# Two-layer kernel: four query and key products moved to the first layer's end, a store handed to the attention, the rotation's second half in fp32r

## The chip, the cores and the metric

The kernel runs on one core of one Trainium2 chip. The metric is the device time in microseconds (us) of one execution; the kernel before takes 1761.54 us, the median of three runs (1761.18 to 1764.38).

## The reference

The input x has 2 sequences of 1024 tokens with 512 features, and all arithmetic is float32. Two layers follow each other:

```
xn = layernorm(x)
x  = x + L0_attn(xn) + L0_ffn(xn)   # L0_attn: rank-8 scan and rank-8 feed-forward
                                    # L0_ffn : fwht(silu(xn@W1.T) * (xn@W3.T)) @ W2.T, hidden size 2048
xn = layernorm(x)
x  = x + L1_attn(xn) + L1_ffn(xn)   # L1_attn: causal attention, 16 heads of 32
                                    # L1_ffn : gated, two of each four hidden values kept
```

`fwht` is a Walsh-Hadamard transform over the 2048 hidden features. As it is linear, the kernel applies it once to W2 instead of to the hidden values: it rotates W2.

## The kernel before

The program is four phases, each ended by a barrier of all engines: `layer_zero` (the whole first layer), `project_qkv` (queries, keys and values of the second), `attention`, and `layer_end`. TensorE has no full-precision product at full rate. So nearly every product is made of three in the format fp32r: an operand a is split into a rounded part (hi) and the rest (lo), and the product is hi·hi + hi·lo + lo·hi. Weights are split on POOL: one instruction rounds, the next subtracts. Activations are rounded on ACT and subtracted on DVE. Everything is written by hand, in order, one program for each engine, with semaphores between them; all DMAs are issued by SP, in order. There is no planner.

**layer_zero.** 2048 tokens are four quarters of 512. A unit u = 4g + t is hidden group g (512 of the 2048 hidden features, in four pieces c) for quarter t. A unit has `hidden` (per c 12 products for the gate and 12 for the other factor), and one unit later `output` (4 tiles of 12 products). At `before_half` TensorE does side work, among it the rotation of W2. Its first half, `rotate`, stores its result to memory (`w_half_turned`); its second half is `turn_down(g, c)` (L369 to L380): 16 products of the 128x128 matrix `turn_w[:, 1]` with a 128x512 block `raw`, in plain fp32, in units 4g+1 before pieces c = 1 and 3. The blocks come through a ring of 3 slots `raw`, which the gate and up weights use too; a slot is refilled when the rotation of it is done. ACT and DVE turn the result into `d_hi` and `d_lo`.

At the end of the layer the normalised rows of quarters 2 and 3 are transposed by `turn_last` (L573), each followed by ACT (x_hi) and DVE (x_lo). Between the two quarters `keep_going(24)` (L558) issues 24 small fp32 products whose result nobody reads.

**project_qkv.** For each of 4 groups of heads ("quads") there are 8 jobs of 12 products: two blocks of 128 rows of the query and key weights (index i) times four quarters of x. ACT evicts a job (`val`, L1247), DVE splits it into `qk` (L1277, L1279), and SP stores `qk` to memory for each two jobs (L1150). The first quad is written out, the other three are a loop; between them stand 16 jobs for the values (L1231), with weights `raw_v` split by POOL (L1201, L1203). At its start this phase loads `raw_w`, `bias`, `scale` and `raw_v`, and POOL splits `raw_w` (L1190, L1193) before the first job. At its end SP waits for both chains of stores of `qk` before it comes to the barrier (L1181).

**attention** loads `stack` from the stored q and k pairs and starts with scores (L1429).

Of the kernel before, what the change touches and what calls it, by code (L numbers as in the profile page):

```python
# [6 lines left out]

# [16 lines left out]
NC = 4  # L24
# [42 lines left out]
def layer_zero(nc, t, ident, x_hi, x_lo, spare, half_turned, parked):  # L67
# [14 lines left out]
    with ExitStack() as ctx:  # L82
# [8 lines left out]
        raw = sb("raw", [P, RING, FLAT])  # L91
# [23 lines left out]
        turn_w = sb("turn_w", [P, 2, P])  # L115
        stats = sb("stats", [P, NT, 6])
# [27 lines left out]
        p_out = ps("p_out", [P, 2, W])  # L144
        p_side = ps("p_side", [P, 2, W])
# [11 lines left out]
        rot_done, rot_copied, tok_normed = sem("rot_done"), sem("rot_copied"), sem("tok_normed")  # L157
        d_turned, d_round, d_split = sem("d_turned"), sem("d_round"), sem("d_split")
# [35 lines left out]
        def _(sp):  # L194
# [92 lines left out]
            for k in range(39, 48):  # L287
                load_raw(k)
            for q in range(QUARTERS):
                store_res(q)  # L290
# [4 lines left out]
        def _(pool):  # L295
            step = Tally(pool_step)

            def split(k, hi, lo):
                landed(pool, k)
                pool.tensor_scalar(hi, raw[:, k % RING], 1.0, 0.0, ALU.mult, ALU.add).then_inc(step.up(), 1)  # L300
                pool.wait_ge(step.sem, step.n)
                pool.tensor_tensor(lo, raw[:, k % RING], hi.bitcast(F32), ALU.subtract).then_inc(raw_split, 1)

# [38 lines left out]
            pool.memset(q_w[:].bitcast(F32), 0.0).then_inc(rows_done, 1)  # L342
            for g in range(1, NG):
                split_gu(g)

        @block.tensor
        def _(pe):
# [227 lines left out]

            tail = (p_gate[:, 0], p_gate[:, 1], p_up[:, 0], p_up[:, 1])
# [515 lines left out]
def project_qkv(nc, wqk, wv, qk_bias, qk_scale, masks, x_hi, x_lo, qk_dram, v_dram, stack, v_first, mask):  # L1092
# [10 lines left out]
    with ExitStack() as ctx:  # L1103
        sb, ps, sem = alloc(nc, ctx)
        raw_w = sb("raw_w", [P, 2, KD, P])
        w_hi = sb("w_hi", [P, 2, KD, P], F32R)
        w_lo = sb("w_lo", [P, 2, KD, P], F32R)
# [8 lines left out]
        qk = sb("qk", [P, 2, 2, S], F32R)  # L1116
        v = sb("v_out", [P, BANKS, QUADS, 4, 2, E], F32R)
        p_job = ps("p_job", [P, BANKS, W])
# [3 lines left out]
        w_loaded = [sem(f"w_loaded{i}") for i in range(2)]  # L1122
        w_rounded = [sem(f"w_rounded{i}") for i in range(2)]
        w_split = [sem(f"w_split{i}") for i in range(2)]
        w_biased = [sem(f"w_biased{i}") for i in range(2)]
        job_done, job_used = sem("job_done"), sem("job_used")
        qk_rounded, qk_split, v_rounded, v_split = sem("qk_rounded"), sem("qk_split"), sem("v_rounded"), sem("v_split")
        qk_stored = [sem(f"qk_stored{i}") for i in range(2)]
# [7 lines left out]
        def _(sp):  # L1136
# [5 lines left out]
            def body(it, last):  # L1142
                if not last:
                    for i in range(2):
                        load_w(it + 1, i)
                for n in range(4):

                    pair = 2 * (n % 2) + n // 2
                    sp.wait_ge(qk_split, QK * it + 2 * n + 2)
                    sp.dma_start(qk_dram[4 * it + pair].rearrange("h p n -> p h n"), qk[:, n % 2].bitcast(F32))\  # L1150
# [28 lines left out]
            for i in range(2):  # L1179
                sp.wait_ge(qk_stored[i], 16 * 2 * QUADS)  # L1180
# [3 lines left out]
        def _(pool):  # L1184
            def split_w(quad, i, first=False):
                pool.wait_ge(w_loaded[i], 16 * (quad + 1))
                if not first:

                    pool.wait_ge(job_done, QK * (quad - 1) + 4 * i + 4)
                pool.tensor_tensor(w_hi[:, i].rearrange("p k m -> p (k m)"), raw_w[:, i].rearrange("p k m -> p (k m)"),  # L1190
                                   one[:, :].to_broadcast([P, D]), ALU.mult).then_inc(w_rounded[i], 1)
                pool.wait_ge(w_rounded[i], quad + 1)
                pool.tensor_tensor(w_lo[:, i], raw_w[:, i], w_hi[:, i].bitcast(F32), ALU.subtract).then_inc(w_split[i], 1)  # L1193
# [3 lines left out]
            for i in range(2):  # L1197
                split_w(0, i, True)
# [10 lines left out]
        def _(pe):  # L1209
            def body(it, first):  # L1210
                for m in range(QK):
                    i = m // 4
                    if m % 4 == 0:
                        pe.wait_ge(w_split[i], it + 1)
                    if not (first and m < BANKS):
                        pe.wait_ge(job_used, QK * it + m + 1 - BANKS)
                    t = m % 4
# [20 lines left out]
        def _(act):  # L1238
            def body(it, first):
                for m in range(QK):  # L1240
                    i = m // 4
                    act.wait_ge(job_done, QK * it + m + 1)
                    if m % 4 == 0:
# [18 lines left out]
        def _(dve):  # L1262
            def body(it, first):
                for m in range(QK):
                    if m in (0, 4):
                        i = m // 4
                        if not first:

                            dve.wait_ge(job_used, QK * (it - 1) + m + 4)
# [6 lines left out]
                    hi, lo = (qk[:, m // 2 % 2, half, part * W:(part + 1) * W] for half in range(2))  # L1276
# [18 lines left out]
def attention(nc, mask, stack, v, ident, qk_dram, v_dram, o_dram, total, o_both, o_stored, load_next):  # L1295
# [40 lines left out]
    with ExitStack() as ctx:  # L1336
        sb, ps, sem = alloc(nc, ctx)
        prob = [sb("prob0", [P, 2, QB, W]), sb("prob1", [P, 2, QB, S])]
# [18 lines left out]
        def width_of(r):  # L1357
            return (r + 1) * P

# [24 lines left out]
        def _(sp):  # L1384
# [26 lines left out]

            for it in range(QUADS - 1):
# [5 lines left out]
        def _(pe):  # L1418
# [15 lines left out]
            def turn(it, h, j):  # L1434
# [6 lines left out]
                for i in range(c0 // P, QB):  # L1441
                    mm = pe.transpose(p_turn[:, (BL * h + j) % TB, i * P:(i + 1) * P],  # L1442
                                      prob[g][:, h % 2, i, kb * P:(kb + 1) * P], ident[:, :])
# [20 lines left out]
        def _(act):  # L1464
            def exp(it, h, r):
# [5 lines left out]
                act.activation(prob[r // QB][:, h % 2, r % QB, 0:width_of(r)], p_score[:, r % 2, 0:width_of(r)], ACT.Exp,  # L1471
# [434 lines left out]
def two_layers(nc, t, out):  # L1906
# [7 lines left out]
    with ExitStack() as ctx:  # L1914
# [6 lines left out]
        phase(nc, layer_zero, t, ident, x_hi, x_lo, spare, half_turned, parked)  # L1921
        total = sb("total", [P, HEADS * NT])
        raw = sb("raw1", [P, RING, KD * P])
        handed = alloc(nc, ctx)[2]
        raw_in = [handed(f"raw1_in{i}") for i in range(RING)]
        o_stored = [handed(f"o_stored{i}") for i in range(4)]

# [4 lines left out]
        with ExitStack() as middle:  # L1932
            sb1 = alloc(nc, middle)[0]
            o_both = sb1("o_both", [2 * E, len(o_stored), W])
            stack = sb1("stack", [P, 2, 2, 2, S], F32R)
            v = sb1("v", [P, B, S // P, 4, 2, E], F32R)
            mask = sb1("mask", [P, 2, P], BF16)
            phase(nc, project_qkv, t["wqk"], t["wv"], t["qk_bias"], t["qk_scale"], t["masks"], x_hi, x_lo, qk_dram,
                  v_dram, stack, v, mask)
            phase(nc, attention, mask, stack, v, ident, qk_dram, v_dram, o_dram, total, o_both, o_stored, load_first_blocks)  # L1940
# [74 lines left out]
```

## Time and profile before

| | |
|---|---|
| median of three runs | 1761.54 us |
| the profiled execution, its own time | 1764.71 us |
| its span, first to last instruction | 1762.5 us |
| TensorE products busy | 1701.5 us, 97% |
| DVE, ACT, POOL busy | 59%, 42%, 14% |
| layer_zero | up to about 642 us |
| project_qkv | about 642 to 788 us |
| attention | about 788 to 1186 us |
| layer_end | about 1186 us to the end |

All times in the document's rows are microseconds from the start of the span. A busy share near 100% says only that products follow each other with little idle time; what is to be gained is in the idle times left, in work on TensorE that is dearer than it has to be, and in work that nobody reads.

### The profile page before, as it was taken

To read this page: it belongs to the slowest core of one execution; us is meant where nothing else is said; L and a number is where in the kernel's file an instruction comes from. 1 tells how busy PE (TensorE), PEld (TensorE's weight loads), DVE (VectorE), ACT (ScalarE), POOL (GpSimd) and SP (SyncE) were. 2 spreads that over 40 slices of the span, in tenths; PEclk is the share of its full clock that TensorE was granted. 3 is DMA by queue.
4 is the path that set the end of the run, shared out by engine and by line. 5 is a ranking of instruction groups with operands and counts; after the bars stand their busy time and mean duration, and the time that the engine had idled before them with its cause. 6 is when DMAs were issued, how large, how long until landed. Compare 5 with 4: busy or idle time off the path is not lost. (4 is left out here: it accounts for less than half of the span.)

```text
span 1762.5 us, 22933 instructions
## 1 busy us (share of the span) xinstructions
PE 1701.5 (97%) x8366; PEld 1370.6 (78%) x8366; DVE 1031.5 (59%) x1795; ACT 735.2 (42%) x1528; POOL 251.8 (14%) x247
## 2 busy tenths in 40 slices
PE   5999999999999979989999999989999999999998
PEld 3777878778788868867777777768888888888887
DVE  4321465464524343348999999974555654655675
ACT  4521322232213322229999999982222222222221
POOL 4001200300300031110000000004144031033230
PEclk9999999999999989999999999999999999999999
DMA  7200110110100036842554445515010010012243
GB/s 291 91 12 1 60 48 19 54 41 15 54 7 25 36 105 231 296 194 64 138 137 122 120 120 166 142 31 171 1 49 24 1 48 25 0 48 57 87 134 130
DMA packets 75663, 149.60 MB, mean 85 GB/s; under 512 B 9497, under 2 KB 26521, under 8 KB 74018
## 3 DMA queue, kind: packets, MB, share of 16 engines
q1 hardware_dynamic: 75554, 148.17, 27.1%
q8 instruction: 65, 1.06, 0.3%
q14 instruction: 44, 0.36, 0.1%
HBM read 101.87 MB, written 46.27 MB: 84 GB/s over the span
## 5 line engine op out<-in xcount | busy, mean ns | idle before, releaser
L1504 DVE TENSOR_TENSOR pt_lo<-p_turn,pt_hi 128x512 fp32r<-128x512 f32 (+3 forms) x384 | 200.9, 551 | 18.9 <-ACT pt_hi L1479 15.0
L1497 DVE TENSOR_REDUCE row_top<-p_score 128x1 f32<-128x128 f32 (+7 forms) x256 | 189.7, 751 | 18.9 <-PE p_score L1431 18.8
L1471 ACT ACTIVATE prob<-p_score,row_top 128x128 f32<-128x128 f32 (+7 forms) x256 | 190.2, 746 | 6.2 <-DVE row_top L1497 5.5
L1479 ACT ACTIVATE pt_hi<-p_turn 128x512 fp32r<-128x512 f32 (+3 forms) x384 | 182.7, 495 | 5.6 <-PE p_turn L1442 1.6
L1442 PE MATMUL p_turn<-ident,prob 128*128 128x128 f32 x1152 | 181.6, 276 | 1.2 <-DVE pt_lo L1504 0.9
L958 DVE TENSOR_TENSOR hid<-hid,p_up 128x512 f32<-128x512 f32 x64 | 44.0, 688 | 221.3 <-PE p_up L435 205.6
L1840 DVE TENSOR_TENSOR e_hid<-e_hid,e_p_up 128x512 f32<-128x512 f32 x64 | 44.0, 688 | 202.9 <-PE e_p_up L1726 202.9
L1457 PE MATMUL p_o<-pt_hi,v 128*128 128x512 f32 (+3 forms) x384 | 148.6, 394 | 3.9 <-ACT o_both L1487 3.1
L1442 PEld LDWEIGHTS p_turn<-ident,prob 128*128 128x128 f32 x1152 | 131.9, 141 | 14.8 <-DVE pt_lo L1504 1.6
L1429 PE MATMUL p_score<-stack 128*128 128x512 f32 (+3 forms) x384 | 128.9, 391 | 10.4 <-PEq L53 7.0
L705 ACT ACTIVATE hid<-p_gate 128x512 f32<-128x512 f32 x64 | 38.3, 598 | 220.3 <-PE p_gate L435 220.2
L1458 PE MATMUL p_o<-pt_lo,v 128*128 128x512 f32 (+3 forms) x384 | 124.8, 346 | 0.0
L1781 ACT ACTIVATE mag<-e_hid 128x512 f32<-128x512 f32 x64 | 40.5, 632 | 184.1 <-DVE e_hid L1840 184.1
L433 PE MATMUL p_gate<-x_hi,gu_hi 128*128 128x512 f32 x256 | 104.9, 410 | 3.6 <-DVE x_lo L851 3.6
L433 PE MATMUL p_up<-x_hi,gu_hi 128*128 128x512 f32 x256 | 105.1, 411 | 0.0
L1724 PE MATMUL e_p_gate<-x_hi,e_gu_hi 128*128 128x512 f32 x256 | 100.8, 394 | 4.4 <-POOL e_gu_lo L1679 4.4
L446 PE MATMUL p_out<-d_hi,h_hi 128*128 128x512 f32 x256 | 100.4, 392 | 0.5 <-DVE res L974 0.5
L1677 POOL TENSOR_SCALAR e_gu_hi<-raw 128x512 fp32r<-128x512 f32 x32 | 22.6, 705 | 546.0 <-POOLq L53 424.9
L1726 PE MATMUL e_p_gate<-x_hi,e_gu_lo 128*128 128x512 f32 x256 | 100.6, 393 | 0.0
L1725 PE MATMUL e_p_gate<-x_lo,e_gu_hi 128*128 128x512 f32 x256 | 100.5, 393 | 0.0
L434 PE MATMUL p_up<-x_lo,gu_hi 128*128 128x512 f32 x256 | 100.0, 391 | 0.0
L435 PE MATMUL p_gate<-x_hi,gu_lo 128*128 128x512 f32 x256 | 100.0, 390 | 0.0
(259 smaller groups left out, 3991.9 us busy)
## 6 DMA issues: line engine op xcount, KB each, us to landing
stack<-qk_parked SPq DMA_DIRECT2D x256, 128.0 KB, 4.0
raw<-in_wgu SPq DMA_DIRECT2D x64, 256.0 KB, 2.6
qk_parked<-qk SPq DMA_DIRECT2D x16, 1024.0 KB, 3.9
v_parked<-v_out SPq DMA_DIRECT2D x16, 512.0 KB, 5.9
v<-v_parked SPq DMA_DIRECT2D x8, 1024.0 KB, 9.7
o_parked<-o_both SPq DMA_DIRECT2D x64, 128.0 KB
res<-in_x SPq DMA_DIRECT2D x8, 512.0 KB
rot<-in_w2t SPq DMA_DIRECT2D x4, 1024.0 KB, 7.4
```

Source lines behind the costliest of these rows:

```text
L433: pe.matmul(acc[:, c % 2], gu_hi[:, c, j, k], x_hi[:, t, k], start=(k == 0), stop=False)
L1429: pe.matmul(p_score[:, r % 2, c0:c1], q, stack[:, pair % 2, a, 1, c0:c1], start=True, stop=c1 < width_of(r))
L1442: mm = pe.transpose(p_turn[:, (BL * h + j) % TB, i * P:(i + 1) * P], prob[g][:, h % 2, i, kb * P:(kb + 1) * P], ident[:, :])
L1457: pe.matmul(p_o[:, c0:W], lhs, pt_hi[:, slot, c0:W], start=(kb == 0), stop=False)
L1458: pe.matmul(p_o[:, c0:W], lhs, pt_lo[:, slot, c0:W], start=False, stop=(j in (QB - 1, BL - 1))).then_inc(weighted, 1)
L1471: act.activation(prob[r // QB][:, h % 2, r % QB, 0:width_of(r)], p_score[:, r % 2, 0:width_of(r)], ACT.Exp, bias=top[:, r:r + 1], accum_ou ...
L1479: act.activation(pt_hi[:, (BL * h + j) % PT, c0:W], p_turn[:, (BL * h + j) % TB, c0:W], ACT.Copy).then_inc(rounded, 1)
L1497: dve.tensor_reduce(top[:, r:r + 1], p_score[:, r % 2, 0:width_of(r)], AX_X, ALU.max, negate=True).then_inc(topped, 1)
L1504: dve.tensor_tensor(pt_lo[:, slot, c0:W], p_turn[:, (BL * h + j) % TB, c0:W], pt_hi[:, slot, c0:W].bitcast(F32), ALU.subtract).then_inc(sp ...
L1724: pe.matmul(acc[:, c % 2], gu_hi[:, c, j, k], x_hi[:, x, k], start=(k == 0), stop=False)
L1725: pe.matmul(acc[:, c % 2], gu_hi[:, c, j, k], x_lo[:, x, k], start=False, stop=False)
L1726: mm = pe.matmul(acc[:, c % 2], gu_lo[:, c, j, k], x_hi[:, x, k], start=False, stop=(k == KD - 1))
```

## The change

**1. The rotation's second half.** `turn_down` waits for POOL instead of for the load, and makes two fp32r products with `turn_r`, a copy of the matrix rounded to fp32r: one with `d_hi[:, c]`, into which POOL has put the rounded block, and one with `half_lo`, the rest, which lies in the ring slot of the block itself.

**2. Four jobs moved.** The first four query and key jobs are done by `layer_zero` in `project(m)`: two behind the transposes of quarter 2, in the place of `keep_going(24)`, and two behind those of quarter 3. Their weights are loaded by SP after the last `turn_down` and split by POOL after the last `hidden`; `project_qkv` neither loads nor splits them, and its first quad starts with job 4. PSUM banks, weight tiles and semaphores are handed over in `Ahead`. The order of the jobs becomes: block 0 on quarters 0 and 1, block 1 on quarters 0 and 1, block 0 on quarters 2 and 3, block 1 on quarters 2 and 3, in all four quads, so POOL may rewrite block 0 after job 5 instead of after job 3.

**3. A store handed on.** SP ends `project_qkv` without waiting for the stores of the second `qk` buffer. Attention's SP waits for them first, and ACT before it writes `o_both`, which lies over that buffer.

**4.** The attention's `prob` is packed into a triangle to make room.

```diff
             def turn_down(g, c):       # TensorE
                 k = d_item(g, c)
-                landed(pe, k)
+                pe.wait_ge(half_split, NC * g + c + 2)
...
-                pe.matmul(p_out[:, c % 2], turn_w[:, 1], raw[:, k % RING], start=True, stop=True).then_inc(d_turned, 1)
+                pe.matmul(p_out[:, c % 2], turn_r[:], d_hi[:, c], start=True, stop=False)
+                pe.matmul(p_out[:, c % 2], turn_r[:], half_lo[:, k % RING], start=False, stop=True).then_inc(d_turned, 1)
...
+            def split_half(g, c):      # POOL
+                k = d_item(g, c)
+                landed(pool, k)
+                if c == 0:
+                    if g:
+                        pool.wait_ge(out_done, J * TT * g)
+                    else:
+                        pool.wait_ge(turned, 3 * KD)
+                hi = d_hi[:, c]
+                pool.tensor_scalar(hi, raw[:, k % RING], 1.0, 0.0, ALU.mult, ALU.add).then_inc(step.up(), 1)
+                pool.wait_ge(step.sem, step.n)
+                pool.tensor_tensor(half_lo[:, k % RING], raw[:, k % RING], hi.bitcast(F32),
+                                   ALU.subtract).then_inc(half_split, 1)
...
             for g in range(1, NG):     # POOL
                 split_gu(g)
+                for c in range(NC):
+                    split_half(g, c)
+            pool.wait_ge(up_done, NC * UNITS)
+            for i in range(2):
+                pool.wait_ge(ahead.loaded[i], 16)
...             (rounds to ahead.hi, rest to ahead.lo)
...
+            def project(m):            # TensorE
+                i, q = m // 2, m % 2
+                if q == 0:
+                    pe.wait_ge(ahead.split[i], 1)
+                if m == 2:
+                    pe.wait_ge(added, J * UNITS)
+                for k in range(KD):
...                 (three products into ahead.bank[:, m])
+                mm.then_inc(ahead.done, 1)
...
             for q in range(2, QUARTERS):
-                if q == 3:
-                    keep_going(24)
                 for k in range(KD):
                     turn_last(q, k, tail[k])
+                for m in range(2 * q - 4, 2 * q - 2):
+                    project(m)
...
-            load_w(0, 0, True)         # project_qkv, SP
             sp.dma_start(bias[:], qk_bias).then_inc(consts, 16)
             sp.dma_start(scale[:], qk_scale).then_inc(consts, 16)
-            load_w(0, 1, True)
...
-            for i in range(2):
-                sp.wait_ge(qk_stored[i], 16 * 2 * QUADS)
+            sp.wait_ge(qk_stored[0], 16 * 2 * QUADS)
...
-                    pool.wait_ge(job_done, QK * (quad - 1) + 4 * i + 4)
+                    pool.wait_ge(job_done, QK * (quad - 1) + 2 * i + 6)
...
-                for m in range(QK):    # project_qkv, TensorE
-                    i = m // 4
+                for m in range(BANKS if first else 0, QK):
+                    i, t = m // 2 % 2, 2 * (m // 4) + m % 2
...
+            sp.wait_ge(*qk_last)       # attention, SP
...
+                if (it, h, g) == (0, 0, 0):      # attention, ACT
+                    act.wait_ge(*qk_last)
```

## Rows read from the trace of the kernel before

**Rows 1.** The page, busy time of each engine: us, share, instructions.

```profile
PE 1701.5 (97%) x8366; PEld 1370.6 (78%) x8366; DVE 1031.5 (59%) x1795; ACT 735.2 (42%) x1528; POOL 251.8 (14%) x247
```

**Rows 2.** Timeline of TensorE around one `turn_down`: start, duration, what; idle time before in brackets.

```profile
532.79 0.39 PE L435 MATMUL p_gate<-x_hi,gu_lo 128*128 128x512 f32 x1
533.02 1.02 PE L380 MATMUL p_out<-raw,turn_w 128*128 128x512 f32 x2
533.47 0.80 PE L433 MATMUL p_up<-x_hi,gu_hi 128*128 128x512 f32 x1
534.11 0.40 PE L434 MATMUL p_up<-x_lo,gu_hi 128*128 128x512 f32 x1
```

**Rows 3.** Tile `raw`, durations min/median/max in ns; then timelines and load landings, 72 to 80.

```profile
L300 POOL TENSOR_SCALAR gu_hi<-raw x32: 612/619/1527, 10.1 to 469.4; 128x512 fp32r<-128x512 f32 x32
L302 POOL TENSOR_TENSOR gu_lo<-raw,gu_hi x32: 1265/1292/1752, 10.8 to 470.5; 128x512 fp32r<-128x512 f32 x32
...
73.61 1.29 SPq L210 DMA_DIRECT2D raw<-w_half_turned  x3
74.97 0.10 POOL L342 MEMSET q_w<- 128x8 f32 x1
76.90 1.02 PE L380 MATMUL p_out<-raw,turn_w 128*128 128x512 f32 x2
...
DMA to landing us min/median/max: 2.7/3.2/3.8
```

**Rows 4.** Timeline of the engines at the end of `layer_zero`.

```profile
631.37 5.52 PE L558 MATMUL p_side<-turn_w,ident 128*128 128x128 f32 x48
633.92 2.93 ACT L625 ACTIVATE res<-res,neg,z_inv 128x512 f32<-128x512 f32 x4
637.00 1.06 PE L573 MATMUL p_gate<-ident,res 128*128 128x128 f32 x8
639.50 1.28 DVE L851 TENSOR_TENSOR x_lo<-p_up,x_hi 128x512 fp32r<-128x512 f32 x2
```

**Rows 5.** Timeline of the engines in the first part of `project_qkv`.

```profile
642.02 0.35 SPq L1140 DMA_DIRECT2D raw_w<-in_wqk  x1
642.89 0.42 SPq L1155 DMA_DIRECT2D scale<-in_qk_scale  x1
643.83 1.85 SPq L1158 DMA_DIRECT2D raw_v<-in_wv  x4
645.54 0.47 DVE L1282 TENSOR_SCALAR bias<-bias,scale 128x8 f32<-128x8 f32 x1 [4.77 <-DMA scale<-in_qk_scale]
646.04 0.15 DVE L1270 COPY pair_bias<-bias 128x1 f32<-128x1 f32 x1
647.38 0.80 PE L1220 MATMUL p_job<-x_hi,w_hi 128*128 128x512 f32 x1 [8.44 <-POOL w_lo L1193]
650.21 0.62 POOL L1201 TENSOR_SCALAR v_hi<-raw_v 128x512 fp32r<-128x512 f32 x1 [0.54 <-DMA raw_v<-in_wv]
652.61 0.78 ACT L1247 ACTIVATE val<-p_job,pair_bias,scale 128x512 f32<-128x512 f32 x1 [12.89 <-PE p_job L1220]
657.45 1.60 POOL L1203 TENSOR_TENSOR v_lo<-raw_v,v_hi 128x512 fp32r<-128x512 f32 x1
671.43 0.39 PE L1231 MATMUL p_v<-v_hi,x_hi 128*128 128x512 f32 x1
```

**Rows 6.** Timeline of POOL in the loop: the split of block 0 for the third quad.

```profile
734.01 1.04 POOL L1190 TENSOR_TENSOR w_hi<-raw_w,one 128x512 fp32r<-128x512 f32 x1 [59.87 <-DMA raw_w<-in_wqk]
735.14 1.29 POOL L1193 TENSOR_TENSOR w_lo<-raw_w,w_hi 128x512 fp32r<-128x512 f32 x1
```

**Rows 7.** Timeline at the end of `project_qkv` and the start of `attention`.

```profile
782.92 0.37 SPq L1150 DMA_DIRECT2D qk_parked<-qk  x1
787.88 0.45 PE L1429 MATMUL p_score<-stack 128*128 128x128 f32 x1 [7.00 <-PEq L53]
```

**Rows 8.** Windows of TensorE: stretch, length, busy (instructions), granted clock, DMA share, GB/s.

```profile
647.38:651.80 4.42, 4.42 (x10) 0.50 0.74 226
```

More of the change, by code:

```diff
@@ L6 @@
 from contextlib import ExitStack
+from dataclasses import dataclass
 import concourse.bass as bass
@@ L64, in up, with layer_zero @@
         return self.sem
-def layer_zero(nc, t, ident, x_hi, x_lo, spare, half_turned, parked):
+@dataclass
+class Ahead:
+    raw: object
+    hi: object
+    lo: object
+    bank: object
+    loaded: list
+    rounded: list
+    split: list
+    done: object
+def layer_zero(nc, t, ident, x_hi, x_lo, spare, half_turned, parked, raw_at, ahead):
     R = 8
@@ L342, in _ @@
             pool.memset(q_w[:].bitcast(F32), 0.0).then_inc(rows_done, 1)
+            pool.wait_ge(turn_in, 16)
+            pool.tensor_scalar(turn_r[:], turn_w[:, 1], 1.0, 0.0, ALU.mult, ALU.add).then_inc(half_split, 1)
+            for c in range(NC):
+                split_half(0, c)
             for g in range(1, NG):
                 split_gu(g)
+                for c in range(NC):
+                    split_half(g, c)
+            pool.wait_ge(up_done, NC * UNITS)
+            for i in range(2):
+                pool.wait_ge(ahead.loaded[i], 16)
+                pool.tensor_scalar(ahead.hi[:, i], ahead.raw[:, i], 1.0, 0.0, ALU.mult, ALU.add).then_inc(ahead.rounded[i], 1)
+                pool.wait_ge(ahead.rounded[i], 1)
+                pool.tensor_tensor(ahead.lo[:, i], ahead.raw[:, i], ahead.hi[:, i].bitcast(F32),
+                                   ALU.subtract).then_inc(ahead.split[i], 1)
         @block.tensor
@@ L1115, in project_qkv @@
         val = sb("val", [P, 2, W])
-        qk = sb("qk", [P, 2, 2, S], F32R)
+        qk = [sb("qk0", [P, 2, S], F32R), qk_parts]
         v = sb("v_out", [P, BANKS, QUADS, 4, 2, E], F32R)
-        p_job = ps("p_job", [P, BANKS, W])
+        p_job = ahead.bank
         p_v = ps("p_v", [P, BANKS, D])
         consts, one_set, scale_done = sem("consts"), sem("one_set"), sem("scale_done")
-        w_loaded = [sem(f"w_loaded{i}") for i in range(2)]
-        w_rounded = [sem(f"w_rounded{i}") for i in range(2)]
-        w_split = [sem(f"w_split{i}") for i in range(2)]
+        w_loaded, w_rounded, w_split, job_done = ahead.loaded, ahead.rounded, ahead.split, ahead.done
         w_biased = [sem(f"w_biased{i}") for i in range(2)]
-        job_done, job_used = sem("job_done"), sem("job_used")
+        job_used = sem("job_used")
         qk_rounded, qk_split, v_rounded, v_split = sem("qk_rounded"), sem("qk_split"), sem("v_rounded"), sem("v_split")
-        qk_stored = [sem(f"qk_stored{i}") for i in range(2)]
         mask_f = sb("mask_f", [P, 2, P])
@@ L1275, in body @@
                         dve.wait_ge(qk_stored[m // 2 % 2], 16 * (2 * it + m // 4))
-                    hi, lo = (qk[:, m // 2 % 2, half, part * W:(part + 1) * W] for half in range(2))
+                    hi, lo = (qk[m // 2 % 2][:, half, part * W:(part + 1) * W] for half in range(2))
                     dve.tensor_copy(hi, val[:, m % 2]).then_inc(qk_rounded, 1)
@@ L1292, in _, with attention @@
                 body(it, False)
-def attention(nc, mask, stack, v, ident, qk_dram, v_dram, o_dram, total, o_both, o_stored, load_next):
+def attention(nc, mask, stack, v, ident, qk_dram, v_dram, o_dram, total, o_both, o_stored, qk_last, load_next):
     G = 2
@@ L1358, in width_of, with row_at @@
             return (r + 1) * P
+        def row_at(h, r, c0, c1):
+            at = r * (r + 1) // 2 * P
+            return prob[:, h % 2, at + c0:at + c1]
         def place_of(h):
```

74 lines of the change are left out of this document (46 added, 28 removed).

## The prediction

> **What bounds the kernel now.** I read the page first: TensorE products are busy for 1701.5 of 1762.5 us [rows 1], so the time is TensorE's own queue, and only three things can shorten it: a cheaper product, a removed one, or an idle stretch filled. DVE (59%), ACT (42%) and POOL (14%) matter where TensorE waits for them. Next I read TensorE's timeline at the places that the diff touches. The reader is to see four things. A rotation is one fp32 product that the profile shows as two records [rows 2]. Between the transposes of quarters 2 and 3 TensorE is filled with 48 records that nobody reads [rows 4]. Behind the first layer it is idle for 8.44 us [rows 5], and before the attention for 7.00 us [rows 7]. After the first of these idle stretches the clock is granted at 0.50, that is 1.2 of 2.4 GHz, for 4.42 us of products [rows 8].
>
> **The base.** An fp32r product of 512 columns follows the one before by 0.23 us [rows 2]. More finely: the 96 products of the first quad take 671.43 - 647.38 = 24.05 us, the first 10 of them 4.42 us at half clock; the other 86 take 19.63 us, 0.228 each [rows 5, 8]. A job of 12 is 2.73 us.
>
> **1. The rotation.** From the product ahead of the rotation (532.79) to the second behind it (534.11) are 1.32 us. Two of the steps in it are ordinary, 2 x 0.23, so the fp32 product costs 0.86 us of the queue. Two fp32r products cost 0.46. Saved: 0.40 each, 16 times, **-6.4 us**. Bounds: TensorE was never shown to make this pair with this weight, but it is the same form as its neighbours, so 0.35 to 0.41 each.
>
> POOL gets 16 pairs of instructions, each 0.62 + 1.29 us plus steps of some 0.05 [rows 3]: 2.0 us a pair, 32 us on an engine that is 86% free. Who waits? For g = 1 to 3 POOL may start when the last output of unit 4g-1 is done, and TensorE then has 24 products (5.5 us) before the first rotation. The pair takes 2.0, the second is needed 3.2 us after the first, the others a good ten us later: no wait. For g = 0 there is no such lead. The loads are issued from 73.61, and land at the earliest 2.7 us later, at 76.3; POOL has been free since 75.1; TensorE asks at 76.90 [rows 3]. The block is split at 76.3 + 2.0 = 78.3, so TensorE waits 1.4 us, once: **+1.4 us** (bounds 0.5, if the load lands at 75.4, and 3.0, if it takes the longest, 3.8, and POOL runs its slower durations). The second rotation finds its block split at 80.3 and asks at 81.5. No DMA is queued behind: slots refill on the same event. DVE is not held up visibly: it waits for TensorE in these units.
>
> The row maximum of the rounding is 1527 ns against a median of 619 [rows 3], so POOL sometimes does stand behind another engine. The Trainium skill says why (SBUF — State Buffer, section "SBUF: two separate sides"): DVE and GpSimd arbitrate for one pair of ports, as an exclusive lock for a whole instruction. By it, up to 32 more instructions of DVE wait for one of POOL. The trace agrees in kind with those 1527 ns. I take nothing for it, since TensorE has PSUM banks in hand; what it would cost if it reached TensorE is rival (b), and the sum by the rule would be that rival's.
>
> **2. The moved jobs.** Before, the fillers start at 631.37 and the transposes of quarter 3 at 637.00, when ACT has the first rows (633.92 + 2.93 = 636.85) [rows 4]. Now two jobs, 5.5 us, stand there: 636.8. The transposes start at 637.0 as before; they are 16, the first 8 shown take 1.06, all about 1.9. Two jobs more, 5.5 us, end at 644.5 with the tail. ACT and DVE end at 640.8 beside them. The weights for these jobs are split by POOL while TensorE makes the last 8 output tiles, 8 x 2.73 = 22 us, for two pairs of 2.0: hidden.
>
> The barrier took from DVE's end, 640.78, to SP's first issue, 642.02: 1.24 us [rows 4, 5]. Now it is passed at 645.7, 3.7 later. There TensorE needs no weights, but bank 0 evicted, and that needs `scale`. Before it was issued third, at 642.89, and used at 645.54, 2.65 later; now it is second, at 646.2, and there at 648.8. DVE takes 0.50 and 0.20 more (645.54, 646.04, end), ACT 0.78 for the job [rows 5]: TensorE starts job 4 at 650.4, where job 0 started at 647.38. So 3.0 are lost and 48 products of 0.228, 10.9 us, are gone: **-7.9 us** at the first product of the values, 663.5 instead of 671.43.
>
> Two covers are to be checked. The four slow microseconds: TensorE is now idle for 5.9 us instead of 8.44. I take the same 4.4 us at half clock, worth 2.1. Bounds: none of it (-2.1), or half as long again (+1). The value weights: `raw_v` is issued from 643.83 on and used at 650.21, 6.4 later, and POOL ends at 659.05 [rows 5]. Now its issue starts at 646.7, POOL starts at 653.1 and ends at 661.9, 1.6 us ahead of 663.5. Before this cover was 12 us; if it fails, TensorE waits the rest.
>
> In the loop POOL may rewrite block 0 two jobs later. For the third quad it was bound by the load anyway, done at 736.4 [rows 6]. TensorE needs it at 671.43 + 16 x 2.73 + 8 x 2.73 = 736.9 or a little later, so 0.5 to 1.1 us of cover, as before. Block 1 is now rewritten after job 7 and needed after two jobs, 5.5 us, where the split takes 2.4 to 2.8. Nothing is lost: 0, bound 2.8 in each of three rounds.
>
> **3. The store.** SP's last store is issued until 783.29 and TensorE starts at 787.88 [rows 7]. Without the wait only the barrier's 1.24 us follow: 784.5, **-3.3 us** (bounds 0 and -3.4). ACT's wait stands before its first write of `o_both`, behind the scores, exponentials and value products of half a head; the store, of which TensorE waited out about 3.3 us before, has landed by then. What is late next is the attention's own start, a chain of score, maximum and exponential that moves as a whole. Packing `prob` changes addresses only: 0.
>
> **Sum.** -6.4 + 1.4 - 7.9 - 3.3 = -16.2. The profiled execution took 1764.71 (span 1762.5), so it would take 1748.5. It was 3.2 above the median of the runs; against 1761.54 I predict **1745.5 us**. Everything behind the attention moves along.
>
> **The rivals.**
> (a) *The covers are too thin.* `raw_v` or `scale` arrives later and the value products wait, or the store's wait gives nothing because the barrier is ended by another engine. For: the cover is 1.6 us where it was 12. Against: fewer transfers compete. It gives back 3 to 6: 1748.5 to 1751.5.
> (b) *The rotations wait for POOL* (the other sign). Place: each of the 15 other rotations. If POOL is always as late as for g = 0, held by DVE or behind the splits of the gate weights, each waits its pair, 2.0: +30, so 1775.5. It decides from about 8 such waits, 16 us. For: POOL's queue is in order and its spread to 1527 and 1752 ns. Against: it has 5.5 us of lead and 2 to do.
> (c) *The loop waits for its weights.* The split after job 7 comes late in three rounds, 3 x 2.8 = 8.4: 1754. Against: 2.7 us of cover.
> (d) *The clock helps.* The idle stretch before the attention shrinks from 7.0 to 3.7, and if the clock isn't lowered there nor behind the first layer, the slow products' 2.1 us go there and, taken as the same, 2.1 at the attention: 1741.3. Against: the attention starts with few and short products, between which TensorE waits.
>
> **How the numbers follow.** Forecast 0.60, (a) 0.16, (b) 0.05, (c) 0.05, (d) 0.10, something I haven't seen 0.04. All but (b) and half of the last are faster by over 0.2% (3.5 us, about what a measurement of this kernel can tell from no change): faster 0.92, same 0.02, slower 0.06. The forecast alone spans 1743 to 1748.5. The range adds (d) and most of (a): 1740 to 1752.
>
> **What would show it.** L380 gone and two products of 0.23 us at each rotation, one wait of about 1.4 us near 77; no further wait for POOL's rest. The fillers gone, 48 products of `project` with no idle time before them, the end of the first layer near 639.5 on the new scale (5 us earlier by the rotations). TensorE idle about 5.9 us there, released by ACT. No idle time before the values. A gap of about 3.7 us before the first score. The prediction is wrong if a wait for POOL shows at more than one rotation, or if the values wait for `v_lo`.

## The result, and the profile after

| | before | after |
|---|---|---|
| median of the runs, in the same comparison | 1761.36 us (1759.36 to 1764.38, 4 runs) | 1744.61 us (1742.82 to 1748.79, 4 runs) |
| ratio after to before | | 0.9902 [0.9887, 0.9917] |
| the profiled execution (its span) | 1764.71 (1762.5) | 1748.79 (1747.0) |

The change takes 16.75 us off the median. 1745.5 us was predicted. Whether its steps were right as well is read from the trace, stretch by stretch. The first view is the line of busy times on the page of the kernel after, which answers to [rows 1]: 48 TensorE records fewer (the 24 fillers, two records each), 33 POOL instructions more (16 pairs, and the rounding of `turn_r`).

```profile
PE 1690.6 (97%) x8318; PEld 1365.9 (78%) x8318; DVE 1044.7 (60%) x1795; ACT 733.9 (42%) x1528; POOL 286.8 (16%) x280
```

The timeline at the first rotation (start, duration, what; in brackets the idle time before and what ended it). It answers to [rows 3]:

```profile
77.26 1.29 SPq L227 DMA_DIRECT2D raw<-w_half_turned  x3
79.94 0.62 POOL L334 TENSOR_SCALAR d_hi<-raw 128x512 fp32r<-128x512 f32 x1 [0.95 <-DMA raw<-w_half_turned]
80.65 1.26 POOL L336 TENSOR_TENSOR half_lo<-raw,d_hi 128x512 fp32r<-128x512 f32 x1
81.96 0.50 PE L428 MATMUL p_job<-d_hi,turn_r 128*128 128x512 f32 x1 [1.26 <-POOL half_lo L336]
```

POOL took the block up 2.68 us after its issue, the pair took 1.97, and TensorE stood for 1.26: step 1's "1.4, once". The timeline of two later rotations, beside [rows 2]:

```profile
526.65 0.39 PE L484 MATMUL p_up<-x_hi,gu_lo 128*128 128x512 f32 x1
526.88 0.39 PE L428 MATMUL p_job<-d_hi,turn_r 128*128 128x512 f32 x1
527.10 0.39 PE L429 MATMUL p_job<-half_lo,turn_r 128*128 128x512 f32 x1
527.33 0.39 PE L482 MATMUL p_gate<-x_hi,gu_hi 128*128 128x512 f32 x1
527.56 0.39 PE L483 MATMUL p_gate<-x_lo,gu_hi 128*128 128x512 f32 x1
...
530.05 0.39 PE L428 MATMUL p_job<-d_hi,turn_r 128*128 128x512 f32 x1
```

From the product ahead to the second behind are 0.91 us where there were 1.32, and no bracket stands anywhere: the weight and the block are there in time.

The timeline at the end of the first layer and the start of `project_qkv`, which answers to [rows 4, 5]:

```profile
626.18 1.04 PE L622 MATMUL p_gate<-ident,res 128*128 128x128 f32 x8
...
627.85 0.47 PE L632 MATMUL p_job<-x_hi,w_hi 128*128 128x512 f32 x1
...
633.56 1.06 PE L622 MATMUL p_gate<-ident,res 128*128 128x128 f32 x8
...
640.60 0.39 PE L634 MATMUL p_job<-x_hi,w_lo 128*128 128x512 f32 x1
...
642.24 0.34 SPq L1208 DMA_DIRECT2D bias<-in_qk_bias  x1
642.63 0.43 SPq L1209 DMA_DIRECT2D scale<-in_qk_scale  x1
643.11 1.85 SPq L1211 DMA_DIRECT2D raw_v<-in_wv  x4
644.72 0.23 DVE L1330 TENSOR_SCALAR bias<-bias,scale 128x8 f32<-128x8 f32 x1 [7.38 <-DMA scale<-in_qk_scale]
645.26 1.45 ACT L1295 ACTIVATE val<-p_job,pair_bias,scale 128x512 f32<-128x512 f32 x2 [8.96 <-DVE pair_bias L1318]
646.09 0.80 PE L1268 MATMUL p_job<-x_hi,w_hi 128*128 128x512 f32 x1 [5.10 <-ACT val L1295]
...
649.36 0.79 POOL L1251 TENSOR_SCALAR v_hi<-raw_v 128x512 fp32r<-128x512 f32 x1 [7.03 <-DMA raw_v<-in_wv]
...
657.42 1.34 POOL L1253 TENSOR_TENSOR v_lo<-raw_v,v_hi 128x512 fp32r<-128x512 f32 x1
657.65 1.65 DVE L1327 TENSOR_TENSOR qk<-val,qk 128x512 fp32r<-128x512 f32 x1
...
658.93 0.40 PE L1279 MATMUL p_v<-v_hi,x_hi 128*128 128x512 f32 x1
```

TensorE is idle for 5.10 us where it was 8.44, and the wait has changed hands: it ends with ACT's eviction, which stands behind `scale`, and no longer with POOL's split. The reader is to see the two last starts as well. The last `v_lo` ends at 657.42 + 1.34 = 658.76, and the first value product starts at 658.93: a cover of 0.2 us, where 1.6 was predicted.

The start of the attention, beside [rows 7]:

```profile
772.48 0.30 PE L1483 MATMUL p_score<-stack 128*128 128x128 f32 x1 [3.48 <-PEq L54]
```

Last, windows of TensorE (length, busy and instructions, granted clock, DMA share, GB/s), which answer to [rows 8]: the first products behind the barrier, and the attention's start.

```profile
643.20:650.00 6.80, 3.91 (x9) 0.50 0.76 253
772.90:783.10 10.20, 7.64 (x28) 0.50 0.16 62
```

From these starts, and the same ones before:

| stretch | before | after | difference |
|---|---|---|---|
| start to the first rotation asked for | 76.9 | 80.7 | +3.8 |
| wait there | 0 | 1.26 | +1.3 |
| first rotation to the transposes of quarter 2 | 552.73 | 544.22 | -8.5 |
| those transposes to the first value product | 41.80 | 32.75 | -9.05 |
| value product to the loop's last job product | 109.07 | 109.67 | +0.6 |
| last job product to the first score | 7.38 | 3.88 | -3.5 |
| first score to the end | 969.89 | 969.61 | -0.3 |

(The transposes of quarter 2 start at 629.63 before and 626.18 after; the end is the start of the last addition to `res`.) The sum is -15.7; the two executions differ by 15.9. The +3.8 is hardly the work of the change. The change edits nothing in that stretch but addresses, and in the nine other kernels below that rotate at the same place (all but r5, r8 and r12) TensorE asks for the first rotation between 74.2 and 77.8. TensorE's waits for `rot` come to the same, 11.0 + 5.1 us in this execution and 9.3 + 6.9 before; what differs is the clock: 13.6 us at half clock fall before 80 instead of 6.8. The -8.5 has 1.55 us of the same kind. Before, the clock is granted at 0.5 from 133.2 to 136.6, behind an idle time of 1.71 us; after, the same idle time stands there and the clock stays at 1.00. The same 12 products behind it take 4.35 us before (from 132.34) and 2.81 after (from 135.77). Half of the kernels below show this slow stretch and half don't, whatever was edited.

### The profile page after: what moved, and what is told of

Its sections match the earlier page's. It is cut to its first block and busy times, and to the rows that moved or that the text cites. A ratio compares the mean times of both kernels' runs of the same rounds, so it can differ in the third digit from the quotient of the medians.

```text
span 1747.0 us, 22877 instructions
## 1 busy us (share of the span) xinstructions
PE 1690.6 (97%) x8318; PEld 1365.9 (78%) x8318; DVE 1044.7 (60%) x1795; ACT 733.9 (42%) x1528; POOL 286.8 (16%) x280
## 5 line engine op out<-in xcount | busy, mean ns | idle before, releaser
L495 PE MATMUL p_job<-d_hi,h_hi 128*128 128x512 f32 x256 | 100.4, 392 | 0.5 <-DVE res L1035 0.5
```

## The experiments

Each kernel is the changed one with the edit shown. Each ratio is against the kernel before, run beside it; the changed kernel's is 0.9902 [0.9887, 0.9917], so an experiment's cost is the difference of the two ratios. 0.001 is 1.76 us, and by the two intervals such a difference is uncertain by about 3.5 us; what is smaller is read from the traces, one execution each.

**r1: the rotation as before.**

```
-                pe.wait_ge(half_split, NC * g + c + 2)
+                landed(pe, k)
...
-                pe.matmul(p_out[:, c % 2], turn_r[:], d_hi[:, c], start=True, stop=False)
-                pe.matmul(p_out[:, c % 2], turn_r[:], half_lo[:, k % RING], start=False, stop=True).then_inc(d_turned, 1)
+                pe.matmul(p_out[:, c % 2], turn_w[:, 1], raw[:, k % RING], start=True, stop=True).then_inc(d_turned, 1)
```

(and POOL's two splits are gone)

> The changed kernel with part 1 alone undone: turn_down makes one plain fp32 product again and POOL splits nothing for it. Theory (the rotation saves 16 x 0.40 = 6.4 us of TensorE's queue and costs one wait of 1.3): 5.1 us slower than the changed kernel, so about 11.5 faster than before; from the first rotation to the transposes of quarter 2 the trace takes 550.6 us against 545.5 of the changed kernel. Rival (the pair is worth the 7.2 us by which that stretch shrank from before): 552.7 us there, as before, and 7.2 slower. Second rival (POOL's 32 more instructions hold DVE up and give part of it back): less than 3 slower.

Measured 1752.04 us, 0.9945 [0.9932, 0.9957], so about 7.6 us slower than the changed kernel; its trace has less, 5.6: from the first rotation to the transposes it takes 552.68 us, and kernels r2, r3 and r7, which keep the new rotation and the same slow stretch at 133, take 545.68, 545.68 and 545.76. That is 7.0 for 16 rotations, 0.44 each, less the one wait of 1.4. The other 2 us lie within what the intervals leave open. The rival's 552.7 is the number that the trace shows, but 1.55 us of it are the slow stretch at 133, which r1 has and the changed kernel has not; net of the wait the rotation gives 5.6, nearer to the theory's 5.1 than to the rival's 7.2. The timeline of r1 behind a rotation shows why 0.44 and not 0.41:

```profile
528.62 1.02 PE L422 MATMUL p_job<-raw,turn_w 128*128 128x512 f32 x2
529.07 0.80 PE L475 MATMUL p_gate<-x_hi,gu_hi 128*128 128x512 f32 x1
529.71 0.40 PE L476 MATMUL p_gate<-x_lo,gu_hi 128*128 128x512 f32 x1
529.94 0.40 PE L477 MATMUL p_gate<-x_hi,gu_lo 128*128 128x512 f32 x1
530.18 0.39 PE L475 MATMUL p_gate<-x_hi,gu_hi 128*128 128x512 f32 x1
...
532.02 0.39 PE L477 MATMUL p_gate<-x_hi,gu_lo 128*128 128x512 f32 x1
532.24 1.02 PE L422 MATMUL p_job<-raw,turn_w 128*128 128x512 f32 x2
```

From 529.71 to 532.24 are 11 steps, 0.230 each, where the changed kernel has 0.2267. From one rotation to the next are 3.62 us, in the changed kernel 3.17.

**r2: the store is waited for again.**

```
-            sp.wait_ge(qk_stored[0], 16 * 2 * QUADS)
+            for i in range(2):
+                sp.wait_ge(qk_stored[i], 16 * 2 * QUADS)
```

> The changed kernel with part 3 alone undone: SP waits for the stores of both qk buffers before the barrier. Theory: the idle time before the first score goes from 3.5 back to 7.0 us and the kernel is 3.4 us slower. Rival (the store's tail is met again in the attention, by the wait before o_both or by the first stack loads): no difference in the whole, within 1 us.

Measured 1749.02 us, 0.9926 [0.9913, 0.9939]: 4.2 slower, in the trace 3.5. The first score of r2:

```profile
773.01 0.45 PE L1484 MATMUL p_score<-stack 128*128 128x128 f32 x1 [7.03 <-PEq L54]
```

From the last job product to this score are 7.42 us instead of 3.88. The attention behind it is as long as in the changed kernel, 400.40 and 400.38 us to the last phase: the store lands under the scores, and nothing is given back.

**r3: the four jobs back in `project_qkv`**, with their loads and splits, and the fillers in their old place.

```
-            for m in range(2 * q - 4, 2 * q - 2):
-                project(m)
+            if q == 3:
+                keep_going(24)
...
+            load_w(0, 0, True)         # project_qkv, SP
...
-                for m in range(BANKS if first else 0, QK):
+                for m in range(QK):
```

> The changed kernel with the four moved jobs back in project_qkv: the fillers, the loads and the splits of the first quad's weights are where they were; the new order of the jobs stays. Theory (48 products of filler time saved, less a barrier 3.6 later and a wait for scale): from the transposes of quarter 2 to the first product of the values 41.5 us against 32.75, and 8.5 to 9 slower in the whole. Rival (part of the gain there comes from a quicker start of the phase by chance, and the order of the jobs in the loop costs something): 6 to 7 slower in the whole and more than 0.5 us of idle TensorE in the loop.

Measured 1753.38 us, 0.9949 [0.9936, 0.9962]: 8.3 slower. Its trace has the old wait again:

```profile
641.65 0.79 PE L1263 MATMUL p_job<-x_hi,w_hi 128*128 128x512 f32 x1 [8.36 <-POOL w_lo L1237]
```

From the transposes to the first value product it takes 41.13 us, the changed kernel 32.75: 8.4. The new order of the jobs stays in r3, and its loop takes 108.85 us against 109.07 before: the order costs nothing. The 0.6 us more in the changed kernel's loop belong to the moved jobs.

**r4: POOL four times as long at the rounding**, three roundings too many for each of the 16 blocks.

```
-                pool.tensor_scalar(hi, raw[:, k % RING], 1.0, 0.0, ALU.mult, ALU.add).then_inc(step.up(), 1)
-                pool.wait_ge(step.sem, step.n)
+                for _ in range(4):
+                    pool.tensor_scalar(hi, raw[:, k % RING], 1.0, 0.0, ALU.mult, ALU.add).then_inc(step.up(), 1)
+                    pool.wait_ge(step.sem, step.n)
```

> The changed kernel, but POOL rounds each block of the rotation four times instead of once: each pair takes 4.0 to 4.1 us instead of 2.0. It measures the lead that POOL has. Theory (5.5 us of lead in g = 1 to 3, none in g = 0): the first rotation waits 3.3 us, the second 0.8, no other: 2.8 us slower than the changed kernel. Rival (the rotations are as close to POOL as the first one): each of 16 waits 2 more, 32 us slower.

Measured 1751.98 us (1748.96 to 1757.65), 0.9947 [0.9931, 0.9963]: 7.9 slower, in the trace 2.1 at the first rotation and 4.3 behind it. A pair on POOL takes 4.1 us or more here. The waits of TensorE in r4 (us in all, times, longest):

```profile
PE p_job L429 <- POOL half_lo L337: 5.2, 3, 3.5
```

Rival (b), a wait at each rotation, would have been over 30 us. The theory's 2.8 was too low as well: the second rotations of groups 0, 1 and 2 start 1.6, 1.0 and 1.0 us later behind their first than in r3 (not all of which the view counts as waits). Two things add up there. POOL's lead is as predicted, which the timeline of the changed kernel shows for group 1:

```profile
230.11 0.62 POOL L334 TENSOR_SCALAR d_hi<-raw 128x512 fp32r<-128x512 f32 x1 [25.13 <-PE p_job L497]
230.81 1.63 POOL L336 TENSOR_TENSOR half_lo<-raw,d_hi 128x512 fp32r<-128x512 f32 x1
235.48 0.39 PE L428 MATMUL p_job<-d_hi,turn_r 128*128 128x512 f32 x1
```

From POOL's start to the rotation are 5.4 us here, 5.4 in group 2 and 5.1 in group 3. But r4's first pair takes 5.0 us in groups 1 and 2 and not 4.1, since three of its four roundings take 0.91 to 0.98 instead of 0.62 beside DVE, and two pairs in a row need 9.5 us where the lead and the 3.2 to the second rotation are 8.6. The real pair takes 2.3 us there and is done 3.0 us ahead of its rotation.

**r5: the first group's blocks one unit later**, so that POOL has its lead there too.

```
+            if u == 1:
+                return [(0, 2 * (c - 2) + j)] if c >= 2 else []
```

> The changed kernel with the four rotations of g = 0 moved 5.5 us later, before pieces 2 and 3 of unit 1 instead of 1 and 3. Theory (the wait of 1.3 us is only the landing of the load): no wait for POOL at any rotation, 1.3 us faster than the changed kernel. Rival (the first output tiles of unit 0 then wait for d_lo of the last piece): the time is the same or up to 2 us slower.

Measured 1745.81 us, 0.9893 [0.9876, 0.991]. No wait for `half_lo` is left in the trace, and none has come in its place, so the rival's doesn't show. The 1.3 us that it should bring are less than this comparison can tell; they are seen in the profile only.

**r6: `bias` and `scale` loaded in the first layer**, so that they are there when the jobs' first eviction wants them. Their tiles are allocated ahead of the ring, which moves all tiles behind `x_hi` and `x_lo` by 64 bytes.

```
+            sp.dma_start(ahead.bias[:], t["qk_bias"]).then_inc(ahead.consts, 16)
+            sp.dma_start(ahead.scale[:], t["qk_scale"]).then_inc(ahead.consts, 16)
...
+        early_bias, early_scale = sb("bias", [P, HEADS // 2]), sb("scale", [P, 8])[:, 0:1]
```

> The changed kernel with bias and scale of project_qkv loaded at the end of the first layer. Theory (the cover of the values' weights is 0.2 us, so an earlier start of the jobs is given back there): job 4 starts 1.3 to 1.6 us behind the phase's first instruction instead of 3.9, but the values start only as much earlier as raw_v is issued, 0.9 us, and TensorE idles about 1.5 us before them, released by v_lo: 0.9 faster. Rival (the jobs alone set the start): 2.4 us faster and no idle time before the values.

Measured 1766.41 us (12 runs), 1.0014 [1.0002, 1.0025]: 20 us slower, which neither theory had. The loss isn't at the edit: 579.77 us from the last phase's first product to the end, where the changed kernel has 569.23. That points at the 64 bytes, which r9 to r11 take apart.

**r7: TensorE kept busy over the barrier**, 16 small fp32 products that nobody reads ahead of job 4.

```
+            for _ in range(16):
+                pe.matmul(p_v[:, 3, 0:P], fill[:, :], fill[:, :], start=True, stop=True)
```

> The changed kernel with 16 small fp32 products, whose result nobody reads, in the idle time of TensorE at the start of project_qkv. They read the identity and write a bank that isn't in use. Theory: the clock stays at 1.00, the four jobs take 10.9 us instead of 12.8, but the values wait for v_lo and start when they did, within 0.3 us: no gain. Rival (the slow clock is what the start costs): 2.0 us faster.

Measured 1747.55 us, 0.9906 [0.9891, 0.992]: no gain. The clock stays at 1.00, and the four jobs are through in 11.2 us instead of 12.8. Then comes, in the timeline,

```profile
655.90 0.80 PE L1281 MATMUL p_v<-v_hi,x_hi 128*128 128x512 f32 x1 [2.37 <-POOL v_lo L1253]
```

and in the windows of TensorE

```profile
655.90:659.00 3.10, 3.10 (x7) 0.50 0.73 301
```

The values wait for POOL, and behind that wait the clock falls after all. The cover of the value weights is used up. "When they did, within 0.3 us" was missed all the same: the values start 18.62 us behind the phase's first issue, where the changed kernel has 16.69, because POOL takes `raw_v` up 8.3 us after its issue and not 6.25.

**r8: r5, r6 and a shorter r7 together**, and ACT rounds the value weights so that POOL only subtracts.

```
-                pool.tensor_scalar(v_hi[:, k], raw_v[:, k], 1.0, 0.0, ALU.mult, ALU.add).then_inc(wv_rounded, 1)
...
+                    if first and m == 3:
+                        act.wait_ge(wv_loaded, 16 * KD)
+                        for k in range(KD):
+                            act.activation(v_hi[:, k], raw_v[:, k], ACT.Copy).then_inc(wv_rounded, 1)
```

> The late first rotations, bias and scale ahead, 6 small products as fillers, and the rounding of the values' weights given from POOL to ACT, behind its fourth eviction, so that POOL only subtracts. Theory: 1.3 from the rotations; POOL's part falls from 9.4 us to 5.3 behind the landing, so the values start when the jobs end: jobs start 2.4 earlier and run warm, another 2.0. Together 5 to 5.5 us faster than the changed kernel. Rival (the landing of raw_v and the order on ACT set the start of the values): only 2 to 3 faster, with an idle time before the values.

Measured 1762.59 us, 0.9995 [0.9985, 1.0004]: 16 us slower than the changed kernel, where both theories had it faster. The barrier to the first value product shrinks from 16.69 to 13.76 us, as meant, and the shift takes all of it and more.

**r9 and r10: only the shift.** One unused tile of 64, then of 128 bytes, behind `x_hi` and `x_lo`.

```
+        sb("pad", [P, 16])             # r9; [P, 32] in r10
```

> The changed kernel with nothing but an unused tile of 64 bytes on each partition, between x_hi, x_lo and all the tiles behind them. Both kernels with bias and scale ahead had such a shift, because these two tiles stood there, and both lost some 6 us in the first layer's second part and 10 in the last phase, where TensorE waits for nothing. Theory (the distance of the weights' address from that of x sets the step of the products in hidden): hidden's products follow each other by 0.233 instead of 0.227 us, those of output keep 0.227, and the kernel is about 20 us slower than the changed one. Rival (it was the earlier loads or the semaphores of those kernels): within 2 us of the changed kernel.

> The same with a tile of 128 bytes. If any shift counts, as slow as with 64 bytes, some 20 us slower than the changed kernel; if the slow step belongs to a distance that is no multiple of 128 bytes, the same as the changed kernel; a third possibility is a faster step than 0.227.

Measured 1767.24 us, 1.0023 [1.0013, 1.0033], and 1765.9 us, 1.001 [1.0001, 1.0019]. A tile that nothing reads makes the kernel some 20 us slower, with 128 bytes about as much as with 64, so a shift by a multiple of 128 bytes is no better. The timeline of r9 in an `output` of the first layer, then in a `hidden` of the last phase:

```profile
539.72 0.39 PE L496 MATMUL p_job<-d_lo,h_hi 128*128 128x512 f32 x1
539.95 0.39 PE L497 MATMUL p_job<-d_hi,h_lo 128*128 128x512 f32 x1
540.17 0.39 PE L495 MATMUL p_job<-d_hi,h_hi 128*128 128x512 f32 x1
540.40 0.39 PE L496 MATMUL p_job<-d_lo,h_hi 128*128 128x512 f32 x1
...
1339.68 0.39 PE L1782 MATMUL e_p_gate<-x_hi,e_gu_lo 128*128 128x512 f32 x1
1339.91 0.39 PE L1780 MATMUL e_p_gate<-x_hi,e_gu_hi 128*128 128x512 f32 x1
1340.15 0.39 PE L1781 MATMUL e_p_gate<-x_lo,e_gu_hi 128*128 128x512 f32 x1
1340.38 0.39 PE L1782 MATMUL e_p_gate<-x_hi,e_gu_lo 128*128 128x512 f32 x1
```

Over six products the first kind takes 0.2267 us a step and the second 0.2333; in the changed kernel both take 0.2267. In the windows of 50 us from 1300 on, r9 has 218 products where the changed kernel has 222 or 223. A phase's 1536 products of `hidden`, 0.0067 us more each, are 10.2 us, and r9's last phase is 9.5 longer. Another 7.5 lie between the first rotation and the transposes, and 2.3 in the loop.

**r11: r6 without the shift**: the two tiles lie in the third slot of the ring, which is free once the last block is rotated.

```
+        early_bias = nc.alloc_sbuf_tensor_at("bias", [P, HEADS // 2], F32, offset=raw0_at + 8 * KD * P)
+        early_scale = nc.alloc_sbuf_tensor_at("scale", [P, 1], F32, offset=raw0_at + 8 * KD * P + 64)
```

> The changed kernel with bias and scale loaded at the end of the first layer into the third slot of the ring, which is free by then: no tile moves. Theory (the cover of the values' weights is 0.2 us): job 4 starts about 1.4 us behind the phase's first instruction, the values start 0.9 us earlier at most, with an idle time of 1.5 to 3 us before them released by v_lo: 0 to 0.9 us faster than the changed kernel. Rival (the jobs set the start of the values): 2.4 faster.

Measured 1750.12 us, 0.9918 [0.9906, 0.9931]. The 20 us are gone, so r6 was slow by its addresses. And the edit by itself doesn't help. In its timeline:

```profile
640.42 1.95 SPq L1214 DMA_DIRECT2D raw_v<-in_wv  x4
641.82 0.76 PE L1271 MATMUL p_job<-x_hi,w_hi 128*128 128x512 f32 x1 [2.65 <-ACT val L1298]
648.84 0.62 POOL L1254 TENSOR_SCALAR v_hi<-raw_v 128x512 fp32r<-128x512 f32 x1 [8.33 <-DMA raw_v<-in_wv]
657.68 0.50 PE L1282 MATMUL p_v<-v_hi,x_hi 128*128 128x512 f32 x1 [3.11 <-POOL v_lo L1256]
```

Job 4 starts 1.4 us behind the barrier instead of 3.9, and the values then wait 3.1: 17.26 us in all, where the changed kernel has 16.69 and r1, r2, r4 and r5, which leave this phase as it is, have 16.7 to 17.7. So not even the theory's 0.9 us came. The clock falls again behind this wait, and the loop takes 111.69 us, 2.0 more. This is the mechanism of rival (a) at full size: take TensorE's wait at the head away, and the next one is the load and split of the value weights.

**r12: r8 without the shift.** `bias` and `scale` as in r11, the rotation as in r5, ACT rounding, 6 fillers.

> The late first rotations, bias and scale ahead in the ring's third slot, 6 small products as fillers, and the rounding of the values' weights on ACT: the combination tried before, without its shift of addresses. Theory: 1.3 us from the rotations and 2.9 between the phase's first instruction and the values, as in that run: 4.2 us faster than the changed kernel, about 1740.5. Rival (the shift was not what cost that run its time): slower than the changed kernel.

Measured 1739.85 us (1738.42 to 1740.92), 0.9861 [0.9847, 0.9875], whose interval lies below that of the changed kernel: 7 us faster than it, 24 faster than the kernel before. The theory had 4.2; the traces show 1.3 at the rotations and 3.35 behind the barrier, and the rest is within what the intervals leave open. The rival (something other than the shift made r8 slow) is out. Its timeline:

```profile
643.71 2.19 ACT L1306 ACTIVATE v_hi<-raw_v 128x512 fp32r<-128x512 f32 x4 [2.06 <-DMA raw_v<-in_wv]
644.52 5.21 POOL L1257 TENSOR_TENSOR v_lo<-raw_v,v_hi 128x512 fp32r<-128x512 f32 x4 [7.99 <-ACT v_hi L1306]
649.78 0.50 PE L1285 MATMUL p_v<-v_hi,x_hi 128*128 128x512 f32 x1 [0.74 <-POOL v_lo L1257]
```

The four pairs, 9.40 us on POOL in the changed kernel, are 6.02 us on two engines, and the barrier (636.44) to the values takes 13.34 us.

## Why the prediction was right, step by step

**1. The rotation** (-6.4 and +1.4). The wait is as predicted: 1.1 to 1.4 us, once, in the eight traces that have this rotation, its order and POOL's usual work. The saving is 7.0, not 6.4: 0.41 is the upper bound that the step gave from one rotation's rows, and another 0.03 comes from a dozen products behind each fp32 product, 0.230 a step instead of 0.2267. The term was 0.6 too small, because it was read between neighbours. A window from one rotation to the next, which the trace of before had, would have held all of it.

POOL's lead of 5.5 us was right (5.1 to 5.4 in groups 1 to 3); the pair takes 2.3 us and not 2.0 in groups 1 and 2, and nothing hangs on it. Of the exclusive lock that the Trainium skill describes (SBUF — State Buffer, section "SBUF: two separate sides") the rotation shows little: POOL's 16 roundings take 615, 618 and 796 ns (least, median, most), its 16 subtractions 1263, 1296 and 1629. Around the moved jobs there is more: DVE's subtraction takes 1.65 us at 657.65 beside POOL, and 0.69 in the loop without it. DVE's busy time grows by 13.2 us with the same 1795 instructions [rows 1], by 5.0 in r3, where the four jobs are back in their old place. The trace agrees in kind with the rule. TensorE's waits for DVE are 11.5 us in all instead of 11.2, but POOL's four pairs of value weights took 9.40 us instead of 8.84 [rows 5].

**2. The moved jobs** (-7.9). Measured -9.05, and +0.6 in the loop behind; r3 gives 8.4. The 48 products of `project` have no wait between them, and SP's first issue behind the barrier comes 1.25 us after the end of the last, as predicted. `scale` was there 2.09 us after its issue instead of 2.65, and DVE's operation took 0.23 instead of 0.47, so that TensorE started 3.9 us behind the barrier's first issue and not 4.7. That is 0.8 of the 1.15; the slow products came to about what was taken. The same 0.8, with POOL's 0.56, is why the cover was 0.2 and not 1.6.

Part of the 1.15 is luck of this execution. From the transposes to the first value product r1, r2, r4 and r5, whose `project_qkv` is the same, take 33.75, 33.61, 33.15 and 32.76 us, so the first part of the step is worth 8.05 to 9.05 by these traces. And in r2, r5 and r9 the first value product starts 0.05 us after the last `v_lo` ends; in r2 TensorE waited 0.4 us for it. That is one of the two signs that the prediction had named for being wrong, at a size too small to matter. So rival (a) was nearer than its 0.16 says: the forecast held, with nothing left beneath it.

The loop didn't wait for weights in any trace, so rival (c) was wrong. Of the loop's +0.6, TensorE's waits for `val` are 0.6 (0.8 instead of 0.2).

**3. The store** (-3.3). Measured -3.5, by r2 +3.5 again.

**4. The clock** (rival (d)). It fell at the attention's start though the idle time was only 3.5 us, and stayed at 0.50 for 10.2 us instead of 13.7; the attention is as long as before, 400.38 against 400.70. Behind the first layer 6.8 us at half clock replace 10.2, but with about as many products in them (9 against 10 [rows 8]), since much of both was idle. By the jobs' lengths 0.3 us is gained: the four jobs take 12.84 us, 1.96 more than 48 steps of 0.2267, and the first quad before took 2.29 more than 96.

With their measured sizes the steps are -7.0 + 1.3 - 9.05 + 0.6 - 3.5 = -17.7. Against it stand -15.7 in the two profiled executions, where chance adds 3.8 at the start and takes 1.55 at 133, and -16.75 in the medians. So -16.2 was 1.5 short of the steps and 0.5 of the medians. That the forecast of 1745.5 came within 0.9 us of the median is in part luck: the ratio alone leaves 2.6 us open to either side, and what the steps gave more than predicted was hidden by the start. (The working itself gives 1748.5 - 3.2 = 1745.3, and the chances for "faster" add up to 0.93, not 0.92; neither matters.) The three parts undone one by one (r1, r2, r3) cost 7.6, 4.2 and 8.3 us by the ratios, 20.1 together where the change gains 17.3, which is within their uncertainty; by the traces they are 5.6, 3.5 and 7.6 (8.4 less the loop's 0.8), 16.7 together. No fourth part is needed.

## What to carry to other kernels

When a wait at the head of a phase is shortened, read how late the next input is by then, and write that cover down in microseconds with its spread: here it fell from 12 us to 0.2, and each further shortening of the head (r7, r11) came back as a wait behind it until that next chain was shortened too (r12). Price a removed instruction over the whole stretch to the next of its kind, not between its neighbours. And in an experiment on one edit keep all other tiles at their addresses: here a tile of 64 bytes hid a change of a few microseconds behind one of 20.

## What was not expected of the hardware

- *A shift of 64 or 128 bytes slows fp32r products.* With `x_hi` and `x_lo` in place and all weights behind them moved by 64 bytes (r9) or 128 (r10), each product of `hidden` follows the one before by 0.2333 us instead of 0.2267, and the kernel is 20 us slower. The products of `output`, whose two operands were moved together, keep 0.2267. The jobs of `project_qkv` step by 0.233 too, and the value products, in which x is the weight, by 0.229 in r9 and 0.233 in r10. Not every shift does this: the change itself puts the ring's 6144 bytes between x and the first layer's weights, and `hidden` keeps 0.2267. That fits a cause in the distance between the weight's and the moving operand's addresses, but no run tried other distances of a few bytes, so the cause stays open. The Trainium skill (TensorE: Matmul & The Clock Gate, section "Wait — 56ns, not 53.3ns?") gives 215.7 ns for a product of 512 columns on a warm engine; no stretch here reached that: with a new weight for each product the step is 0.2267 us at granted clock 1.00.
- *An fp32 product slows those behind it.* After it, some dozen fp32r products step by 0.230 us and not 0.2267, though they use other operands (r1).
- *The same load is there after 6.25 to 8.4 us.* `raw_v` is used by POOL 6.25 us after its first issue in the changed kernel, 6.6 to 7.1 in r1, r2, r4 and r5, where nothing around it was edited, and 8.42 in r11, where it is issued first and no load of `bias` and `scale` goes ahead. It takes 8.3 in r7 too, where those loads do go ahead. What held it there isn't settled.
